# A two-layer kernel with a selective scan: small powers and the last states' weighing moved to ScalarE and TensorE, dt's product made from half-precision rows

## The reference, cut to what matters

```python
proj = hidden_states @ W_in.T
x, gate = (proj[..., :D_IN], proj[..., D_IN:])          # D_IN = 1024
...                                                      # causal convolution of 4 taps
x = jax.nn.silu(xc)
ssm = x @ W_x.T
ts, Bm, Cm = (ssm[..., :R], ssm[..., R:R + N], ssm[..., R + N:])   # R = 32, N = 16
ts, Bm, Cm = rms_forward(ts), rms_forward(Bm), rms_forward(Cm)
dt = jax.nn.softplus(ts @ W_dt.T + b_dt)
A = -jnp.exp(A_log.astype(jnp.float32))
def step(state, inp):
    dt_t, B_t, C_t, u_t = inp
    dA = jnp.exp(dt_t[..., None] * A)
    state = state * dA + (dt_t * u_t)[..., None] * B_t[:, None, :]
    y = jnp.einsum('bdn,bn->bd', state, C_t)
    return (state, y)
...
y = (ys + x * D) * jax.nn.silu(gate)
return y @ W_out.T
```

## Time and profile before

| | |
|---|---|
| three runs | 1514.06, 1514.07, 1514.89 us |
| profiled execution, its own time | 1512.44 us |
| its span, first to last instruction | 1510.3 us |
| mean granted TensorE clock | 0.959 |
| busy over the span: TensorE | 1349.8 us (89%) |
| VectorE | 1213.1 us (80%) |
| GpSimd | 1028.2 us (68%) |
| ScalarE | 952.1 us (63%) |

### The profile page before, as it was taken

One profiled execution on the slowest core, in us unless ns is written; L12 is line 12 of the kernel. 1 busy time (PEld: TensorE's weight loads), 2 busy tenths in 40 slices (PEclk: granted clock), 3 DMA queues, 4 the chain that ended last, 5 costly groups with the idle time before them and its releaser, 6 DMA issues.

```text
span 1510.3 us, 25293 instructions
## 1 busy us (share of the span) xinstructions
PE 1349.8 (89%) x8817; PEld 1006.2 (67%) x8817; DVE 1213.1 (80%) x1643; ACT 952.1 (63%) x2617; POOL 1028.2 (68%) x697
## 2 busy tenths in 40 slices
PE   6899999999999959699899899899899999988677
PEld 5566677768776748568668667667766766855543
DVE  5794674556443469999999999999999999999994
ACT  3432343233321577788888897798798888886761
POOL 0353242313212398998998999899899899899870
PEclk9799999999999979899999999999999999999689
DMA  9531222101100200100110110020030020020001
GB/s 331 195 112 37 91 79 84 56 29 36 36 29 15 87 18 1 57 29 15 57 42 1 57 57 1 31 83 1 15 99 1 15 86 14 1 71 29 1 1 42
DMA packets 32388, 77.16 MB, mean 51 GB/s; under 512 B 3667, under 2 KB 4723, under 8 KB 31750
## 3 DMA queue, kind: packets, MB, share of 16 engines
q1 hardware_dynamic: 32262, 75.55, 15.1%
HBM read 66.99 MB, written 8.55 MB: 50 GB/s over the span
## 4 chain that ended last, share of the span: by engine, by line
PE 31%; POOL 13%; DVE 12%; ACT 6%; issue 5%; DVEq 0%; ACTq 0%; POOLq 0%
PE ps_h L1502 10%; DVE h L2273 7%; POOL h L2131 7%; POOL dbu L2097 6%; PE ps_m L1466 4%; DVE acc L2289 3%; ACT ps_a L1757 2%; PE ps_o L1526 2%; PE ps_m L165 2%; PE ps_s L1466 2%; PE ps_m L166 2%; PE ps_m L167 2%; PE ps_m L1426 2%; ACT ab L1889 1%; PE ps_s L165 1%
## 5 line engine op out<-in xcount | busy, mean ns | idle before, releaser
L2273 DVE TENSOR_TENSOR_SCAN h<-ps_a,dbu 128x512 f32<-128x512 f32 x512 | 595.8, 1205 | 21.3 <-ACT ps_a L1757 7.1
L2097 POOL TENSOR_TENSOR dbu<-dtu,b_all 128x1020 f32<-128x1020 f32 x256 | 598.3, 2358 | 14.4 <-DVE h L2273 13.9
L1757 ACT ACTIVATE ps_a<-dt,a_neg 128x256 f32<-128x256 f32 (+1 forms) x1024 | 442.9, 466 | 67.7 <-DVE h L2273 66.6
L1502 PE MATMUL ps_h<-ident,h 128*128 128x128 f32 x1536 | 226.4, 290 | 65.3 <-DVE acc L2289 60.0
L2289 DVE SCALAR_TENSOR_TENSOR acc<-ps_h,c_cur,acc 128x512 f32<-128x512 f32 x384 | 267.9, 737 | 16.9 <-PE ps_h L1502 16.3
L1502 PEld LDWEIGHTS ps_h<-ident,h 128*128 128x128 f32 x1536 | 183.1, 149 | 123.0 <-DVE h L2273 82.4
L724 POOL TENSOR_TENSOR hid_l<-hid,hid_h 128x256 f16<-128x256 f32 (+1 forms) x88 | 77.4, 883 | 155.0 <-ACT hid_h L610 154.8
L2131 POOL TENSOR_TENSOR h<-h,c_all 128x1024 f32<-128x1024 f32 x64 | 151.1, 2362 | 19.2 <-ACT carry L1777 19.2
L602 ACT ACTIVATE sil<-ps_gu 128x256 f32<-128x256 f32 (+1 forms) x88 | 33.9, 385 | 180.6 <-PE ps_gu L167 180.6
L165 PE MATMUL ps_m<-h_h,wi_h 128*128 128x256 f16 x432 | 119.4, 276 | 2.6 <-PEq L155 2.4
L166 PE MATMUL ps_m<-h_l,wi_h 128*128 128x256 f16 x432 | 119.2, 276 | 0.0
(11 more groups left out here) (406 smaller groups left out, 2876.8 us busy)
## 6 DMA issues: line engine op xcount, KB each, us to landing
b_all<-bt_scratch SPq DMA_DIRECT2D x32, 512.0 KB, 3.9
wm<-in_wmod SPq DMA_DIRECT2D x7, 1024.0 KB, 5.2
wo<-in_wmod SPq DMA_DIRECT2D x5, 1024.0 KB, 8.6
xa<-in_x SPq DMA_DIRECT2D x8, 512.0 KB, 4.5
stage<-in_W_in SPq DMA_DIRECT2D x4, 1024.0 KB
x_scratch<-x SPq DMA_DIRECT2D x8, 512.0 KB, 3.1
c_all<-bt_scratch SPq DMA_DIRECT2D x8, 512.0 KB, 6.0
x<-x_scratch SPq DMA_DIRECT2D x8, 512.0 KB, 3.6
```

Source lines behind the costliest of these rows:

```text
L1502: tr = pe.transpose(ps_h[:, t, j * P:(j + 1) * P], h[:, s % RING, j, t * P:(t + 1) * P], W["ident"][:])
L1757: ex = nc.scalar.activation(ps_a[:, j, j % 2:], dt[:, m, j % 2:], ACT.Exp, scale=a_neg[:, m, st:st + 1])
L2097: nc.gpsimd.tensor_tensor(dbu[:, s % AHEAD, :, 1:], dtu[:, :, 1:], b_all[:, st, 1:].unsqueeze(1).to_broadcast([P, DG, CH - 1]), ALU.mult). ...
L2273: nc.vector.tensor_tensor_scan(h[:, s % RING, two].rearrange("p j t -> p (j t)"), ps_a[:, two].rearrange("p j t -> p (j t)"), dbu[:, s % A ...
```

## The change

1. **Small powers.** `rms_pow` (GpSimd) becomes `rms_root` (ScalarE): Ln and Exp, behind `join_acc` in `others` of step 21. `inv_std_a` becomes five small ScalarE operations in `others` of step 24. The table load that both need moves from step 23 to step 20. The first chunk keeps GpSimd's.
2. **Last states.** State 15 of each group is no longer added by VectorE. `weigh_last_state` (ScalarE) multiplies `ps_h` by C into a buffer that is free, and `turn_y` adds it by four more transposes that accumulate in `ps_s`. TensorE's next group waits for the copy (`last_weighed`), not for the add.
3. **dt's product.** The turned ts lie three times on the partitions, in half precision: rows 0 to 31 high part, 32 to 63 the rest (one product with `minus_mid` subtracts the rounded part), 64 to 95 high part again. W_dt is scaled by 64 and laid out as high, high and low part. One half-precision product a tile replaces the full-precision one. `tsb_in` has three copies now and waits once for TensorE.
4. **Places.** `make_y(4)` and `make_y(6)` go from steps 1 and 2 to 2 and 3, `turn_y(6)` and `out_projection(2)` from step 1 to 2, `turn_y(4)` behind `gate_tile(7)`, `dt_add(i, 1)` from step 7 to 12, `first_decay(i, 1)` from 8 to 10, `d_u(i, 1)` from 10 to 12, `old_state` behind the first operation of `first_inputs`.

```diff
-YB_AT = {0: (4,), 1: (6,)}
+YB_AT = {0: (4,), 2: (6,)}
+MAKE_YB_AT = {2: (4,), 3: (6,)}
-WO_AT = {0: (1,), 1: (2,), 3: (3,), 4: (4,), 6: (5, 6), 7: (7,)}
+WO_AT = {0: (1,), 2: (2,), 3: (3,), 4: (4,), 6: (5, 6), 7: (7,)}
...
+DT_ADD_AT = 12
...
+        def weigh_last_state(i, g):
+            act.wait_ge(S["c_done"], i + 1)
...
+            for t in range(TT):
+                act.wait_ge(S["hT_done"], turned_at(i, use_of_step((g + 1) * NS - 1), t))
+                nc.scalar.activation(last_of[g][t], ps_h[:, t], ACT.Copy, scale=c_cur[:, t, NS - 1:NS]).then_inc(S["last_weighed"], 1)
...
+            if s == NS - 1:
+                weigh_last_state(i, 0)
...
+                elif not first:
+                    weigh_last_state(i - 1, NDG - 1)
...
-                elif (st == 0 or st > JOIN_AT + 2) and not (first and s == 0):
-                    add_state(i if s else i - 1, (s - 1) % STEPS)
+                elif st > JOIN_AT + 2:
+                    add_state(i, s - 1)
...
+        def rms_root(n):
+            act.wait_ge(S["ms_done"], n * 2 + 2)
+            nc.scalar.activation(mse[:], msq[:], ACT.Ln, bias=rms_eps[:]).then_inc(S["me_done"], 1)
+            act.wait_ge(S["me_done"], n + 1)
+            nc.scalar.activation(rms[:], mse[:], ACT.Exp, scale=-0.5).then_inc(S["rms_done"], 1)
+
+        def inv_std_a(n):
...
+            nc.scalar.activation(veps[:], var_a[:], ACT.Ln, bias=W["epsilon"][:, 0:1]).then_inc(S["inv_a"], 1)
+            act.wait_ge(S["inv_a"], n * 3 + 1)
+            nc.scalar.activation(rstd[:], veps[:], ACT.Exp, scale=-0.5).then_inc(S["inv_a"], 1)
+            act.wait_ge(S["inv_a"], n * 3 + 2)
+            for t in range(TT):
+                op = nc.scalar.activation(nm[:, t:t + 1], nms_a[:, at + t:at + t + 1], ACT.Copy, scale=rstd[:, t:t + 1])
+            op.then_inc(S["inv_a"], 1)
+            act.wait_ge(S["inv_a"], n * 3 + 3)
+            nc.scalar.activation(nmr[:], nm[:], ACT.Copy, scale=ROOT).then_inc(S["nmr_a"], 1)
...
             if m == 0:
-                pe.wait_ge(S["tsb_done"], n + 1)
+                pe.wait_ge(S["ts_done"], n * 2 + 1)
+                pe.matmul(ps_s[:, 0:CH], minus_mid[:], ts[:], start=False, stop=True, skip_group_check=True).then_inc(S["ts_sub"], 1)
                 pe.wait_ge(S["gate_sg"], n * KI + 2)
+                pe.wait_ge(S["ts_done"], n * 2 + 2)
...
-            pe.matmul(dt_bank(m), w_dt[:, m * P:(m + 1) * P], tsb[:], start=True, stop=True)\
+            pe.matmul(dt_bank(m), w_dt[:, m * P:(m + 1) * P], ts[:], start=True, stop=True)\
...
-            if s == 7:
-                dt_add(i, 1, first)
             if p is not None and s == 12:
                 inv_std_b(p)
+            if s == (7 if first else DT_ADD_AT):
+                dt_add(i, 1, first)
```

More of the change, by code:

```diff
@@ L1278, in _ @@
         sp.wait_ge(S["pad_done"], 1)
-        sp.dma_start(w_dt[0:RDT, :], A["W_dt"]).then_inc(S["w1_loaded"], 16)
-        sp.dma_start(w_dt[ONE_ROW:ONE_ROW + 1, :], A["b_dt"]).then_inc(S["w1_loaded"], 16)
+        for at in range(3):
+            sp.dma_start(w_dt_in[at * RDT:(at + 1) * RDT, :], A["W_dt"]).then_inc(S["w1_loaded"], 16)
+        sp.dma_start(w_dt_in[ONE_ROW:ONE_ROW + 2, :], A["b_dt"].to_broadcast([2, DI])).then_inc(S["w1_loaded"], 16)
         def load_xa(n):
@@ L1508, in turn_y @@
             if m % DG == 0:
-                pe.wait_ge(S["hT_used"], added_at(i, NS - 1 if m == 0 else STEPS - 1, TT - 1))
+                pe.wait_ge(S["hT_used"], added_at(i, NS - 2 if m == 0 else STEPS - 2, TT - 1))
             for j in range(2):
                 for t in range(TT):
-                    tr = pe.transpose(ps_s[:, j * CH + t * P:j * CH + (t + 1) * P], acc[:, t, (m + j) * P:(m + j + 1) * P], W["ident"][:])
+                    pe.matmul(ps_s[:, j * CH + t * P:j * CH + (t + 1) * P], acc[:, t, (m + j) * P:(m + j + 1) * P], W["ident"][:],
+                              is_transpose=True, start=(j == 0 and t == 0), stop=False, skip_group_check=True)
+            if m % DG == 0:
+                pe.wait_ge(S["last_weighed"], last_weighed_at(i, m // DG, TT - 1))
+            for j in range(2):
+                for t in range(TT):
+                    at = (m % DG + j) * P
+                    tr = pe.matmul(ps_s[:, j * CH + t * P:j * CH + (t + 1) * P], last_of[m // DG][t][:, at:at + P], W["ident"][:],
+                                   is_transpose=True, start=False, stop=True, skip_group_check=True)
             tr.then_inc(S["y_mm"], 1)
@@ L1617, in iteration @@
                     gate_tile(i, 6)
+                if s == 0 and not first:
+                    gate_tile(i, 7)
                 if p is not None:
@@ L1620, in iteration @@
                         turn_y(p, m)
-                if s == 0 and not first:
-                    gate_tile(i, 7)
                 if n is not None:
@@ L1868, in dt_abs @@
             top = dt[:, m:m + 2] if m < DG else relu[:, m - DG:m - DG + 2]
-            nc.scalar.activation(top, two, ACT.Relu)
-            nc.scalar.activation(ab[:, m:m + 2], two, ACT.Abs).then_inc(S["dt_abs"], 2)
+            nc.scalar.activation(top, two, ACT.Relu, scale=1.0 / WS)
+            nc.scalar.activation(ab[:, m:m + 2], two, ACT.Abs, scale=1.0 / WS).then_inc(S["dt_abs"], 2)
         def dt_decay(n, g):
@@ L1973, in others @@
                 d_u(i, 0)
-            if s == 8:
+            if s == (8 if first else 10):
                 first_decay(i, 1)
-            if s == 10:
+            if s == (10 if first else 12):
                 d_u(i, 1)
@@ L2011, in others @@
                         dt_abs(n, m)
-                if s == 23:
+                if s == WX_AT + 3:
                     nc.scalar.preload_act_table_set("natural_log_exp_and_others")
-                    if p is not None:
-                        router_exp(p)
-                        router_share(p)
+                if s == WX_AT + 4:
+                    rms_root(n)
+                if n < LASTC and s == RA_AT + 7:
+                    inv_std_a(n)
+                if s == 23 and p is not None:
+                    router_exp(p)
+                    router_share(p)
                 if s == 25:
@@ L2121, in first_inputs @@
             op.then_inc(S["fold_done"], 1)
+            if g and n:
+                old_state(n, g)
             pool.wait_ge(S["fold_done"], (n * 2 + g) * 3 + 2)
@@ L2208, in others @@
                 inv_std_a(0)
-            if n is not None and n < LASTC and s == RA_AT + 7:
-                inv_std_a(n)
-            if s == 7:
-                dt_add(i, 1, first)
             if p is not None and s == 12:
                 inv_std_b(p)
+            if s == (7 if first else DT_ADD_AT):
+                dt_add(i, 1, first)
             if p is not None and s == RA_AT + 6:
@@ L2218, in others @@
                 weigh(p)
-            if s == 12:
+            if first and s == 12:
                 old_state(i, 1)
@@ L2235, in iteration @@
                     weigh_h(i, s - (AHEAD - 1))
-                if n is not None and s == WX_AT + 5:
-                    rms_pow(n)
                 others(i, p, n, first, s)
-        nc.gpsimd.memset(w_dt[:], 0.0).then_inc(S["pad_done"], 1)
+        nc.gpsimd.memset(w_dt_in, 0.0).then_inc(S["pad_done"], 1)
         for m in (4, 6, 5, 7):
@@ L2245, in _ @@
         rms_pow(0)
[L2246 removed]
+        pool.wait_ge(S["begun"], 7)
         first_inputs(0, 0)
```

91 lines of the change are left out of this document (66 added, 25 removed).

## The result

The changed kernel takes 1529.25 us (median of 4 runs, 1528.08 to 1531.38), the kernel before 1514.48 us in the same comparison (4 runs, 1514.06 to 1515.46). The ratio on record is 1.0108, 95% interval 1.0094 to 1.0122: slower by 15 us by the medians and 16 by the ratio, where 9 were forecast. The direction and most of the steps held; the size was too small.

A forecast was written before the change was run, and what follows sets the result against it. The bound was taken to be a ring of tight links across engines, not VectorE alone. A stride grows 1.3 us (0.5 to 2.2), six give 7.8, plus 1.2 makes 9.0: forecast 1523 us, range 1504 to 1530.

The forecast's parts named there:

- Step A: Steps 15 to 17: ScalarE's two copies delay the carry and GpSimd's weighing of state 16; +0.9 us (+0.7 to +1.1).
- Step B: Steps 16 to 21: GpSimd runs without a gap and passes the delay on, ending at 970.4 instead of 969.50.
- Step C: Step 22: the power now follows the join on ScalarE, so the scan of step 23 shifts by +1.0 us.
- Step D: Steps 23 to 29: ScalarE late by another 0.2 to 0.4 us; dt's logarithm moves by +1.2.
- rival 3: Step 20: the table load takes longer at its new place, making the kernel slower; chance 0.03.
- Step E: Steps 29 to 6: GpSimd's last weighing +1.2 us, TensorE's add_h behind the late y(6) +1.4; the later counts.
- Step F: Steps 6 to 15: first_decay waits for GpSimd's sum, 0.85 us late; TensorE hides most, counted as +0.1.
- The first and the last chunk with the tail: Outside the six strides: step A there and W_dt's preparation ahead of the first chunk, together 1.2 us, an estimate.
- What is taken away: Per stride: VectorE loses 2.7 us, GpSimd about 3; TensorE loses 3.7 on dt's product, gains about 2.1 by transposes.
- Rival 1: Faster: if state 16's carry isn't later, a stride loses up to 2.7 us, 17 in all, 1497; chance 0.24.
- Rival 2: No change: GpSimd's 1.6 us saving in step 22 cancels the delay at state 15; 1511 to 1517, chance 0.16.
- Rival 4: TensorE's clock makes the kernel slower; chance 0.04.

The follow-up runs named there:

- b_last_alone: Kernel before with only the last states' weighing moved to ScalarE and TensorE (item 2), all other places old; ratio 1.0052 (1.0032 to 1.0072).
- b_copy_late: Changed kernel with item 4's places undone and the copies of state 15 behind the carry of state 16; ratio to before 1.0034 (1.0018 to 1.0050).

## Why the prediction was right in direction and short in size

- **Step A held.** Two copies take 1.26 us from first to last, 0.59 from start to start (0.6 taken). From the turn of state 15 to the weighing of state 16 it is 3.70 us, before 2.85: +0.85 against +0.9. b_last_alone and b_copy_late show it by itself, from both sides.
- **Step B held**: GpSimd's 16.22 us without a gap.
- **Step C** is 0.85 instead of 1.0: no more than GpSimd's shift. VectorE's wait of 0.99 for `rms` was foreseen.
- **Step D held**: 0.27 up to dt's sum, 0.2 to 0.4 forecast. The table load took 1.28 us and the next instruction started 1.29 behind it, so rival 3 is out; no run shows a longer load, each one behind the first scan takes 1.28 us in all 18 profiles.
- **Step E** nearly held: VectorE's wait of 1.64 for the carry, TensorE's of 0.84 for y(6). From the turn of state 15 to the next join 1.54 us were lost, forecast were 1.2 to 1.4.
- **Step F failed.** "TensorE hides most of it; I count +0.1": it hides a third. ScalarE waits 1.45 us for the sum behind `inv_std_b`, VectorE then 0.89 for ScalarE, and TensorE 0.29 for VectorE. Of the 0.85 us of lateness that had been worked out there 0.57 are left at the turn of state 15; alone the move costs 0.62, undone it gives 0.6 back in the same stride. The step wrote it off against an engine that was gapless, but TensorE waits for ScalarE's and VectorE's results within one step, and a stretch without a gap is no cover when what it waits for comes late.
- **Missing from the sum**: behind the late turned input ScalarE waits 1.33 us in step 5, the scan of step 6 comes late, and the add of state 4 with it: 0.23 a stride. It is the other end of the late y(6), past the join at which the prediction stopped following it.
- In sum a stride grew by 2.37 instead of 1.3, which is 6.4 us in six, and just above the 2.2 of the upper bound. The bounds don't follow from the steps: A from 0.7 to 1.1, C with 0.1, D from 0.2 to 0.4, E up to 0.2 and F with 0.1 make 1.1 to 1.9, not 0.5 to 2.2. The first and the last chunk with the tail gave 2.0 instead of 1.2 in the first profile and 0.4 in the second, so this term can't be judged.
- **What is taken away** held for VectorE and GpSimd (112.1 and 107.9 us a stride, 111.6 and 107.6 forecast), less for ScalarE (102.3, forecast 104.5), and not for TensorE, which was to lose 1.6 us and gained 0.8 (107.83 to 108.67); dt's product itself did fall, from 5.0 to 1.8 (two tiles, from their start to that of what follows, from 0.87 to 0.22, the quarter that was taken), and why the total rose all the same stays open.
- **Rival 1 fell**, and for the reason given: its condition, the carry of state 16 not later, isn't met. b_copy_late met it and still wasn't faster than before.
- **Rival 2 fell**: between the weighing of state 16 and the scan of step 23 nothing was won back (12.41 and 12.41).
- **Rival 4** (TensorE's clock) didn't come: in steps 22 to 25 the changed kernel has the lower clock once or twice a stride, 0.50 for 3.4 us at a time (6.8 in one place), as the kernel before has, and it doesn't last through the expert products in any. But it isn't free there. In each profile of the changed kernel one stride is 0.7 to 0.8 us longer than the shortest (121.04 and 121.11 us), and the time is lost in step 22 of the one and step 23 of the other, where the granted clock is 0.71 and 0.68. In the kernel before the longest stride is 0.3 over the shortest. Other clock drops came in step 6 of some of the experiments (0.76 to 0.84 over the step).

## What to carry to other kernels

An engine that is gapless in a stretch is a cover only for work that it doesn't wait for within that stretch: ask of each delay who consumes it and how soon, before it is put at nothing. Where two ways meet in one wait, write down both lengths; taking work off one of them gives nothing, and moving work later on the other costs only what it goes beyond the first, so that costs measured alone don't add up. And a part that takes 2% of an engine's work away (VectorE here) can cost time, if the engine that takes it over stands ahead of the one operation for which a gapless chain waits.
